# Column maxima of a quantised linear layer: one transpose per column chunk instead of folds over four tiles

## The reference

```python
def _smooth_quant_linear(x, w):        # x [T, D], w [O, D]
    amax_x = jnp.max(jnp.abs(x), axis=0)          # maxima by column
    amax_w = jnp.max(jnp.abs(w), axis=0)
    s = jnp.sqrt(jnp.maximum(amax_x, EPS) / jnp.maximum(amax_w, EPS))
    xs, ws = x / s, w * s
    x_scale = jnp.maximum(jnp.max(jnp.abs(xs), axis=-1, keepdims=True), EPS) / QMAX
    w_scale = jnp.maximum(jnp.max(jnp.abs(ws), axis=-1, keepdims=True), EPS) / QMAX
    x_q = jnp.clip(jnp.round(xs / x_scale), -QMAX, QMAX)
    w_q = jnp.clip(jnp.round(ws / w_scale), -QMAX, QMAX)
    return x_q @ w_q.T * x_scale * w_scale.T

x = _layernorm(x + attention(x))                  # 16 heads
h = _smooth_quant_linear(x, fside[b])             # D = 512, O = 512
gate, up = jnp.split(h, 2, axis=-1)
y = _smooth_quant_linear(silu(gate) * up, ctx[b]) # D = 256, O = 512
x = _layernorm(x + y)
x = _layernorm(x + mixture_of_experts(x))         # 16 routed experts, 4 of them per token, and 2 shared ones
```

## Time and profile before

| | us |
|---|---|
| median of 3 runs | 1454.87 |
| lowest and highest | 1453.15 to 1462.58 |
| the profiled execution | 1448.41 |
| its span | 1446.4 |
| mean granted clock of TensorE, share of full | 0.962 |

### The profile page before, as it was taken

The page is one execution under the profiler, slowest core; times in us unless marked ns, Lnnn a source line. Parts: engine busy times, 40 slices in busy tenths (PEclk is TensorE's granted clock), DMA queues, the critical chain, the costliest instruction groups (busy, mean ns, idle before and its releaser), DMA issues.

```text
span 1446.4 us, 24161 instructions
## 1 busy us (share of the span) xinstructions
PE 1314.7 (91%) x7375; PEld 984.3 (68%) x7375; DVE 867.7 (60%) x1455; ACT 439.0 (30%) x651; POOL 402.7 (28%) x495
## 2 busy tenths in 40 slices
PE   7998899989898999889999998999999999879991
PEld 3554445445544555478978887999999988768891
DVE  2443877587758776887668875334433445465534
ACT  1132243414441254232211013223322334353423
POOL 1131013200240015000103832344433444333432
PEclk9999999999999999999999999999999999989996
DMA  8441533233521533504110005445454466768447
GB/s 291 127 100 38 166 86 101 75 119 87 147 75 44 131 103 88 175 20 149 67 36 30 30 29 176 85 79 140 96 119 85 96 149 155 190 183 238 75 75 256
DMA packets 89593, 163.14 MB, mean 113 GB/s; under 512 B 8528, under 2 KB 29520, under 8 KB 89440
## 3 DMA queue, kind: packets, MB, share of 16 engines
q1 hardware_dynamic: 72640, 121.83, 27.2%
q0 software_dynamic: 16816, 39.59, 14.7%
HBM read 112.37 MB, written 49.02 MB: 112 GB/s over the span
## 4 chain that ended last, share of the span: by engine, by line
PE 71%; DVE 14%; DMA 5%; issue 5%; ACT 3%; SPq 1%; DVEq 1%; POOL 1%; ACTq 0%; POOLq 0%
PE psR L1140 14%; PE psUA L1040 12%; PE psUB L1040 11%; PE psY L1047 8%; PE psR L1047 5%; PE psOT L1261 4%; PE psR L1230 3%; PE psST L1244 3%; PE psTX L1023 2%; PE psTH L1056 2%; DMA room<-in_L_ffn_w_dram 2%; PE psR L1154 2%; DVE nm L1639 2%; DVE w_s L1317 1%; DVE xs L1555 1%
## 5 line engine op out<-in xcount | busy, mean ns | idle before, releaser
L1040 PE MATMUL psUA<-w_s,xgT 128*128 (+1 forms) x1284 | 243.1, 340 | 8.1 <-DVE xgT L1437 4.0
L1040 PE MATMUL psUB<-w_s,xgT 128*128 (+1 forms) x1284 | 225.5, 325 | 0.0
L1040 PEld LDWEIGHTS psUA<-w_s,xgT 128*128 128x128 f32 x1284 | 213.8, 196 | 14.4 <-issue 5.5
L1040 PEld LDWEIGHTS psUB<-w_s,xgT 128*128 128x128 f32 x1284 | 211.4, 190 | 0.0
L852 POOL DMA_INDIRECT sx_d<-yg,dst_i x74 | 119.4, 1614 | 302.7 <-ACT yg L930 269.6
L892 ACT ACTIVATE silg<-psUA 128x352 f32<-128x352 f32 x107 | 49.5, 462 | 402.3 <-PE psUB L1040 402.3
L1047 PE MATMUL psY<-w_s,hgT 128*128 (+3 forms) x621 | 160.8, 403 | 0.2 <-issue 0.2
L1446 DVE SCALAR_TENSOR_TENSOR hg<-silg,cws,psUB 128x352 f32<-128x352 f32 x75 | 43.5, 580 | 175.3 <-ACT silg L892 175.3
L814 POOL TENSOR_SCALAR_AFFINE_SELECT pT<-pT 128x128 f32<-128x128 f32 (+1 forms) x192 | 61.3, 336 | 297.2 <-ACT pT L970 297.0
L1639 DVE TENSOR_REDUCE nm<-psR 128x1 f32<-128x128 f32 (+3 forms) x256 | 111.8, 486 | 38.9 <-PE psR L1232 35.9
L1047 PEld LDWEIGHTS psY<-w_s,hgT 128*128 128x128 f32 (+1 forms) x621 | 112.6, 189 | 22.0 <-issue 0.4
(11 more groups left out here) (229 smaller groups left out, 1911.6 us busy)
## 6 DMA issues: line engine op xcount, KB each, us to landing
room<-in_L_ffn_w_dram SPq DMA_DIRECT2D x32, 704.0 KB, 5.9
scr_d<-qhl SPq DMA_DIRECT2D x32, 512.0 KB, 3.8
qst<-scr_d SPq DMA_DIRECT2D x48, 256.0 KB, 4.1
kst<-scr_d SPq DMA_DIRECT2D x48, 256.0 KB, 6.1
room<-in_L_ffn_w_dram SPq DMA_DIRECT2D x16, 512.0 KB, 7.5
xt<-in_x_dram SPq DMA_DIRECT2D x4, 1024.0 KB, 7.7
xr<-in_x_dram SPq DMA_DIRECT2D x4, 1024.0 KB, 5.2
breg<-in_fside_BxS2xS_dram SPq DMA_DIRECT2D x4, 1024.0 KB, 8.5
```

Source lines behind the costliest of these rows:

```text
L1040: mm = pe.matmul(t[:, 0:F], xgT[:, par, a_, c * P:(c + 1) * P], w[:, buf, b_, c, :], start=(c == 0 and n == 0), stop=(c == C - 1 and n == ...
```

## The change

The steps `wfold` and `xfold` go, and with them the tiles `wm`, `xm` and their semaphores. `wtr` and `xtr` become one step for each chunk of 128 columns: TensorE transposes the chunk of all four tiles into one bank (four transposes, 512 columns), and VectorE reduces that bank to one number per partition. Per batch that is 8 + 4 steps with 48 transposes and 12 reductions of [128, 512], where there were four steps with 12 transposes, four reductions of a bank and four folds. The tables `SEQ` and `ending` are written in other orders; `SEQ` has four fillers where it had six, `ending` eight as before.

```diff
-            return ([("wtr", n), ("xtr", n), ("s", n)] + [("wfold", 1)] * (n == 0) + [("sr", n)]
+            return ([("wtr", n, c) for c in range(cn)] + [("xtr", n, c) for c in range(cn)] + [("s", n), ("sr", n)]
...
-        b_steps = [("wfold", 0), ("stat", 0), ("ln1",), ("xfold",)] + quant_steps(0, C) + [("a2",), ("gate",)] + quant_steps(1, C2) + [
+        b_steps = [("stat", 0), ("ln1",)] + quant_steps(0, C) + [("a2",), ("gate",)] + quant_steps(1, C2) + [
...
-            "xt:0 xt:1 fill:1 xt:2 xt:3 fill:2 wfold:0 stat:0 ln1 xfold qk:0 wtr:0 qk:1 xtr:0 s:0 wfold:1 sr:0 v:0 "
+            "xt:0 stat:0 ln1 xt:1 xt:2 fill:0 xt:3 qk:0 wtr:0:0 wtr:0:1 wtr:0:2 wtr:0:3 xtr:0:0 xtr:0:1 xtr:0:2 "
+            "xtr:0:3 s:0 sr:0 qk:1 ws:0 wtop:0 qk:2 qk:3 wq:0 v:0 v:1 wb:0 wqt:0:0 fill:1 max:0 wqt:0:1 max:1 fill:3 "
...
-                    elif kind == "wtr":
-                        pe.wait_ge(s_wm, 2 * b + n + 1)
-                    elif kind == "xtr":
-                        pe.wait_ge(s_xm, 2 * b + n + 1)
+                    elif x == ("wtr", 0, 0):
+                        pe.wait_ge(s_bw, 32 * b + 32)
+                    elif kind == "xtr" and c == 0:
+                        pe.wait_ge(s_qin, 2 * b + n + 1)
...
-                    elif kind in ("wtr", "xtr"):
-                        top = wm if kind == "wtr" else xm
-                        for m in range(C2 if n else C):
-                            mm = pe.transpose(t[:, m * P:(m + 1) * P], top[:, m * P:(m + 1) * P], ident[:, :])
+                    elif kind == "wtr":
+                        mm = transposes(t, wc if n else wf, c)
+                    elif kind == "xtr":
+                        mm = transposes(t, h1 if n else x1, c)
...
-                def largest(top, src, signal):
-
-                    dve.tensor_reduce(top[:, 0:src.shape[2]], src.rearrange("p i n -> p n i"), AX.X, ALU.max,
-                                      apply_absolute_value=True).then_inc(signal, 1)
...
-                        done(dve.tensor_reduce(am[:, 0:cn], t[:, 0:w].rearrange("p (m j) -> p m j", m=cn), AX.X, ALU.max,
-                                               apply_absolute_value=True))
+                        done(dve.tensor_reduce(am[:, x[2]:x[2] + 1], t, AX.X, ALU.max, apply_absolute_value=True))
...
                         dve.tensor_tensor(gate_half, gate_half, h1[:, :, I2:D], ALU.mult).then_inc(s_qin, 1)
-                        dve.wait_ge(s_qin, 2 * b + 2)
-                        largest(xm, gate_half, s_xm)
```

More of the change, by code:

```diff
@@ L133, in decoder_layer @@
         s_col = sem("s_col")
-        s_wm = sem("s_wm")
-        s_xm = sem("s_xm")
         s_quant = sem("s_quant")
@@ L171, in decoder_layer @@
         SEQ = [step(word) for word in (
[9 rows of a table removed]
-            "wo:2 route:3 wo:3 ").split()]
[9 rows of a table added]
+            "bc:2 bc:3 lgt route:0 route:1 wo:0 route:2 wo:1 route:3 wo:2 wo:3 ").split()]
         assert [x for x in SEQ if x[0] in B_KINDS] == b_steps
@@ L274, in decoder_layer @@
         ending = [("ready",)] + [step(word) for word in (
[6 rows of a table removed]
-            "route:1 ha:7:0 hb:7:0 route:2 ha:7:1 route:3 hb:7:1 ").split()]
[7 rows of a table added]
+            "hb:7:1 ").split()]
         assert [x for x in ending if x[0] in B_KINDS] == b_steps
@@ L303, in decoder_layer @@
         x1 = sb("x1", [P, ST, D])
-        wm = sb("wm", [P, D])
         xs = sb("xs", [P, ST, D])
@@ L326, in decoder_layer @@
         gate_half = h1[:, :, 0:I2]
-        xm = xs[:, 0, :]
         gw = h1[0:E, 0, :]
@@ L1654, in walk @@
                         done(dve.tensor_tensor(xr[:, n, :], xr[:, n, :], t, ALU.add))
-                    elif kind == "wfold":
-                        dve.wait_ge(s_dfree, at.freed(x))
-                        if n == 0:
-                            apart(dve)
-                            dve.wait_ge(s_bw, 32 * b + 32)
-                        largest(wm, wc if n else wf, s_wm)
                     elif kind == "stat":
@@ L1670, in walk @@
                         normalise(xr, s_qin)
-                    elif kind == "xfold":
-                        after()
-                        apart(dve)
-                        dve.wait_ge(s_qin, 2 * b + 1)
-                        largest(xm, x1, s_xm)
                     elif kind in ("wtr", "xtr"):
                         am = amw if kind == "wtr" else amx
-                        done(dve.tensor_reduce(am[:, 0:cn], t[:, 0:w].rearrange("p (m j) -> p m j", m=cn), AX.X, ALU.max,
-                                               apply_absolute_value=True))
+                        done(dve.tensor_reduce(am[:, x[2]:x[2] + 1], t, AX.X, ALU.max, apply_absolute_value=True))
                     elif kind == "s":
```

## The result

The changed kernel takes 1445.4 us (median of 16 runs, 1437.6 to 1452.8) against 1458.6 (16 runs, 1447.5 to 1462.6) for the one before: a ratio of 0.9918, 95% interval 0.9901 to 0.9935, some 12 us less (the two medians as they stand lie 13.2 apart). The forecast was 14 less.

A forecast was written before the change was run, and what follows sets the result against it. TensorE, busy for 91% of the span, was taken as the bound. Terms of -11.2 us for three passes, -1.0 for the first and -1.8 for the ending gave -14.0, from a median of 1454.9 to 1441; range 1432 to 1465.

The forecast's parts named there:

- Transposes and fillers: Per batch 36 more transposes, +11.6 us in three passes; two fillers fewer per pass, -2.6 in three passes.
- The waits before xtr:0: TensorE's waits for VectorE's fold at the top of the three passes (4.2, 3.4, 2.5) go: -10.1 us.
- The stretch in their place: Eight bank reductions on VectorE pace TensorE's transposes at the top; it idles 2.0 us per pass: +6.0.
- The slow clock behind them: The slow-clock stretch behind `xtr:0` in the three passes goes: -4.4 us.
- The clock at the top: Clock might fall among the eight banks of transposes: 7.5 us if in every pass; half taken, +3.8.
- The rival in which the clock falls at the top: Clock falls at the top of every pass, costing 7.5 us instead of 3.8: 1445 us; chance 0.12.
- Small waits: Old waits in `max:0`, behind `a2` and in `max:10` go, -13.1 us; new ones of 2.6 per pass, +7.8.
- scores:8: New wait for the row maxima: 3.7 us of `weigh` cover about 4 of cast and load, leaving 0.5 us.
- The slow stretch in the middle: The 9.4 us at clock 0.64 behind the rounding of the gated tile go, 3.4 per pass: -10.2 us.
- a clock that falls at a new place: Named as the main way to be wrong: one wait of some 2 us among transposes costs another 3 per pass.
- the rival: Slow clock mid-pass stays, as the rounding can hold `max:12` for up to 1.8 us: 1453 us; chance 0.20.
- First pass and ending: First pass: two fillers less and a slightly better place for `qk:5`, -1.0 us; ending: folds go, -1.8 us.

The follow-up runs named there:

- twice: Changed kernel with every bank of transposes of the column maxima written two times: 1458.5 us, ratio 1.0024 to the kernel before.
- trans_wait: Changed kernel with three fillers, each four transposes instead of four products, added between weigh:7 and scores:8: 1440.9 us, ratio 0.9885 to the kernel before.
- again: Changed kernel without an edit, run for a second trace: 1446.0 us, ratio 0.9926 to the kernel before.
- chunks_old: Changed kernel's code (chunks, no folds) with the orders of passes and ending of the kernel before: 1462.1 us, ratio 1.0041 to the kernel before.
- old_passes: Changed kernel with its new ending, but the steps of the passes in the order of before: 1453.2 us, ratio 0.9981 to the kernel before.
- before_again: Kernel before without an edit, run for a second trace: 1456.3 us, ratio 0.9997 to the kernel before.

## Why the prediction was right, and where not

The time was forecast as 14.0 us less and came as 12. The forecast's share of clock, -10.8, is what all runs together show (-10.7), but that is in part luck: it took +3.8 for a loss at the top that is not there, and had no term for the loss at scores:8 that is. Of the other -3.2 (three passes -0.4, first pass -1.0, ending -1.8) all runs show only -0.3.

**Transposes and fillers**, +11.6 and -2.6 in three passes: their pace is 0.43 for four as assumed. By twice, 5.2 us of them more cost 3.1 at full clock.

**The waits before xtr:0**, -10.1, went completely. The stretch in their place, estimated at 3.4 + 2.0, is 5.3 to 5.5 us in every pass. The slow clock behind them, -4.4, went too; it was 5.1 and 8.5 in the two traces of before (the 1.1 that the prediction had for one pass is too low: over some 5.8 us, as in the second turn, it is 1.5 to 1.7 in each).

**The clock at the top.** Here the sum took +3.8, half of what a fall in every pass would cost. That step was wrong: the clock is 1.00 in every turn. The rule of the Trainium skill ("TensorE: Matmul & The Clock Gate", "Part 4: PE-mode transpose", that a transpose does not count as busy time for the clock as a product does) does not hold for these transposes in float32: 7.0 us of them alone kept 2.4 GHz in twice, and the clock held in three passes of three with twelve of them in the wait in trans_wait. The rival in which the clock falls at the top (1445) gives the right time for a reason that is not there.

**Small waits**, -13.1 + 7.8. The old ones are gone. Of the new ones, `max:0` was put at 0.5 and is 0 in the turns (1.10 and 0.99 in the pass written out), `xtr:1` at 0.3 and is 0.65 with the wait ahead of it (364.51 and 369.93 above), the last maxima at 0.8 and are 0.8, `max:12` at 0.5 and is 0.2. `scores:8` is the step that failed: "3.7 us of weigh behind rows:2, for a cast on VectorE behind xs and a small load, about 4: 0.5". From the transpose of the maxima to their arrival it is 4.7 to 5.9 us (390.36 to 395.84 above), and the wait 0.87 to 2.08. The new waits of the second turn add up to 3.3 us, against the 2.6 forecast.

**The slow stretch in the middle**, -10.2. The one behind the rounding went as forecast. But what was said of it, that the clock is lost behind a single wait of some 2 us, then happened at scores:8 in half the passes, for 10 to 17 us instead of 9.4: it gave back 8.5 and 5.1 in the two traces, and `max:0` another 3.4 in the first of them. The prediction named this ("a clock that falls at a new place") without a chance of its own, and had the rival look for it at the rounding.

**First pass and ending**, -1.0 and -1.8. The first pass was 121.0 and 131.2 us in two traces of before, 127.4 and 132.2 in two of the changed kernel; at full clock that is 121.0, 117.5, 118.6 and 118.4, so no change of 1.0 can be read from it. The ending gained 0.3 and lost 1.1 in two traces; TensorE waits longer at its start in the new order. TensorE's and VectorE's orders of time there, of again:

```profile
608.11 2.79 PE L1151 MATMUL psR<-ident,breg 128*128 128x128 f32 x12 [6.41 <-DVE psTH L1605]
```

```profile
607.48 0.48 DVE L1605 MEMSET psTH<- 128x512 f32 x1 [0.18 <-DVE xr L1646]
```

TensorE's first wait there is 6.4 us, where both traces of before have 3.8 ahead of the waits of the earlier trace rows. It is 3.8 and 3.9 in chunks_old and old_passes, and 6.3 to 6.4 in the other kernels with chunks and the new passes (4.8 to 5.2 in twice and those with fillers), whichever ending they have: the order of the passes brings VectorE to `psTH` later. That it is the place of `route:3`, which has moved, was not tested. The longer wait took 2.5 of the 3.3 that the folds' end was to give.

Taken together: without its clock the forecast is -10.1 + 6.0 + 11.6 - 2.6 - 13.1 + 7.8 = -0.4 for three passes, and the traces have 443.0 and 442.3 before, 440.3 and 442.2 after: -1.4. With it, -10.8 more were forecast, and 20.5 and 18.7 lost became 18.4 and 8.4: -6.2 in these traces. All runs together say it more sharply, with 10.7 of clock and 0.3 of the rest: the gain of this change is clock, and that waits were shortened is paid for by the products that took their place. What remains open is what share of the 12 us of the medians each pass has: two traces of each are few, the experts' part, which the change does not touch, loses 27 to 34 us of clock of its own in them, and one pass differs by up to 10 us between two executions (160.1 and 149.8 for the one written out).

## What to carry to other kernels

When an engine is busy over 90% of the time, look at what its waits do to the clock before you look at their length: one pause of 1 to 2 us was followed by up to 8.5 us lost, and three useless fillers in it were worth some 5 to 9 us (ratios of 0.9856 to 0.9887 in the four kernels that have them), where the whole change was worth 12. A removed operation and the order that was built around it go together: try the edit alone and the order alone, for each may lose what both win. And take a second trace of the kernel before, since a lucky one hides what the change has to beat; the mean clock of every timed run tells whether it was.

## What the runs showed of the hardware

The clock does not fall by the length of a wait alone: behind one of 2.07 us it held and behind one of 1.50, at the same place in the program, it fell for 10 us. A fall cost from 1.7 to 8.5 us. Such falls are most of the scatter from run to run: lost clock and span have a correlation of 0.81 over the 71 runs of before, 0.93 over the 22 of the changed kernel and 0.95 over the 12 of old_passes, whose times lie between 1444 and 1460. The trace of old_passes, the fastest of its runs, lost 10 us of clock up to the experts' part, where that of before_again (1455.2) lost 39. Transposes of [128, 128] in float32 run at 0.11 us each (64 in 7.0 us), and the clock stayed at 2.4 GHz while TensorE did nothing else for 7.0 us.
